# Two group norms whose statistics are taken where the image is written, and weights loaded by two queues

## The reference

```python
def _gn(v, G=16, eps=1e-5):
    g = v.reshape(B_, G, C_ // G, H_, W_)
    m = jnp.mean(g, axis=(2, 3, 4), keepdims=True)
    s = jnp.var(g, axis=(2, 3, 4), keepdims=True)
    return ((g - m) / jnp.sqrt(s + eps)).reshape(v.shape)

x = x + _L0_conv_ref(_gn(x), ...)   # attention over 16,384 pixels, one head of 48 channels
x = x + _L1_conv_ref(_gn(x), ...)   # 1x1 conv to 288 channels, 8x8 patch Fourier filter, 3x3 depthwise, GELU gate, 1x1
x = x + _L2_conv_ref(_gn(x), ...)   # state space scan over 4096 tokens of 192 features
x = x + _L3_conv_ref(_gn(x), ...)   # box means at learned offsets
```

## Time and profile before

| | |
|---|---|
| median of 3 runs | 7481.2 us (7479.07 to 7481.92) |
| profiled execution, its own time | 7482.72 us |
| its span in the trace | 7480.9 us |
| attention, units | 315 to 3119 us |
| block of the norm ahead of layer 1 (`gn1`) | 3121.9 to 3146.4 us |
| patch filter | 3146.4 to 3632.0 us |
| block of the norm ahead of layer 2 (`gn2`) | 3632.4 to 3657.9 us |
| DVE busy | 6842.5 us, 91% |
| PE busy | 6171.0 us, 82% |
| ACT busy | 5235.5 us, 70% |
| POOL busy | 3435.1 us, 46% |

### The profile page before, as it was taken

The page is one execution under the profiler, slowest core; times in us unless marked ns, Lnnn a source line. Parts: engine busy times, 40 slices in busy tenths (PEclk is TensorE's granted clock), DMA queues, the critical chain, the costliest instruction groups (busy, mean ns, idle before and its releaser), DMA issues. The chain is left out here.

```text
span 7480.9 us, 170231 instructions
## 1 busy us (share of the span) xinstructions
PE 6171.0 (82%) x69312; PEld 2683.0 (36%) x69312; DVE 6842.5 (91%) x6229; ACT 5235.5 (70%) x5309; POOL 3435.1 (46%) x1811
## 2 busy tenths in 40 slices
PE   6899999999999999799668888888888888866330
PEld 3333333333333333366323333333333333333220
DVE  7799999999999999899779999999999999986776
ACT  3388888888888888633468888888888888842000
POOL 2000000000000000100169999999999999974777
PEclk9899999999999999899889999999999999987665
DMA  2200000000000000000110000000000000022333
GB/s 42 61 8 8 8 11 8 8 8 8 8 11 8 8 8 8 4 0 0 45 49 6 6 6 6 6 6 6 6 6 6 6 6 6 6 57 74 83 84 81
DMA packets 129089, 146.51 MB, mean 20 GB/s; under 512 B 52077, under 2 KB 111245, under 8 KB 127261
## 3 DMA queue, kind: packets, MB, share of 16 engines
q1 hardware_dynamic: 102848, 82.30, 4.1%
q0 software_dynamic: 24576, 50.36, 2.6%
q10 hardware_dynamic: 960, 3.74, 0.3%
HBM read 98.55 MB, written 37.75 MB: 18 GB/s over the span
## 5 line engine op out<-in xcount | busy, mean ns | idle before, releaser
L1753 POOL TENSOR_TENSOR k_image<-k_image,s_b 128x1024 f32<-128x1024 f32 x1152 | 2700.6, 2355 | 117.9 <-ACT k_image L1666 83.3
L705 ACT ACTIVATE att_prob<-att_scores,a_bound,a_temp 128x1024 f32<-128x1024 f32 x2048 | 2354.8, 1201 | 421.9 <-PE att_scores L648 421.9
L716 DVE TENSOR_TENSOR att_prob_lo<-att_prob 128x1024 f16<-128x1024 f32 x2048 | 2431.9, 1237 | 157.3 <-ACT att_prob L705 141.7
L633 POOL TENSOR_TENSOR k_image<-k_image,att_rden 48x512 f32 x32 | 67.7, 2115 | 2987.5 <-DVE att_rden L728 2987.5
L1666 ACT COPY k_image<-h_du 128x1024 f32<-128x1024 f32 x1152 | 1166.2, 1012 | 322.5 <-PE h_du L1600 321.9
L1716 DVE TENSOR_TENSOR_SCAN h_state_odd<-h_keep,k_image 128x1024 f32<-128x1024 f32 x576 | 1366.2, 2470 | 0.0
L648 PE MATMUL att_scores<-att_queries,att_keys 32*128 32x512 f16 (+1 forms) x20480 | 1294.2, 378 | 21.4 <-DMA att_queries<-qk_halves 18.8
L1672 ACT ACTIVATE h_keep<-h_keep,h_decay 128x1024 f32<-128x1024 f32 x1152 | 1256.7, 1091 | 74.7 <-PE h_keep L1589 51.0
L665 PE MATMUL att_sums<-att_prob,a_values 128*64 128x512 bf16 x8192 | 1125.4, 395 | 0.0
L1589 PE MATMUL h_keep<-h_rows,h_spread 128*128 128x512 bf16 x2304 | 698.8, 385 | 511.8 <-DVE h_state_odd L1716 263.2
L1600 PE MATMUL h_du<-h_rows,h_spread 128*128 128x512 bf16 x2304 | 701.2, 386 | 37.0 <-DMA h_rows<-parts 34.8
(11 more groups left out here) (296 smaller groups left out, 7026.6 us busy)
## 6 DMA issues: line engine op xcount, KB each, us to landing
y_rows<-h_y_sb SPq DMA_DIRECT2D x1024, 3.0 KB
att_queries<-qk_halves SPq DMA_DIRECT2D x124, 128.0 KB, 2.2
parts<-t_part SPq DMA_DIRECT2D x48, 192.0 KB, 2.5
h_rows<-parts SPq DMA_DIRECT2D x128, 72.0 KB
b_shared<-cells,b_index POOLq DMA_INDIRECT x512, 2.6
qk_halves<-qkv_hi SPq DMA_DIRECT2D x128, 48.0 KB, 1.6
cells<-b_shared SPq DMA_DIRECT2D x4, 1536.0 KB, 5.1
att_keys<-qk_halves SPq DMA_DIRECT2D x32, 128.0 KB, 3.0
```

What stands on the lines that cost most here:

```text
L705: nc.scalar.activation(prob[:, u % RING, :], scores[:, u % SLOTS_S, :], ACT.Exp, bias=bound[:, 0:1], scale=temp[:, 0:1]).then_inc(prob_rea ...
L716: nc.vector.tensor_tensor(prob_lo[:, u % RING, :], prob[:, u % RING, :], prob_hi[:, u % RING, :], ALU.subtract).then_inc(low_ready, 1)
L1753: nc.gpsimd.tensor_tensor(drive[k % 3], du_sb[k % 3], b[:, c * CH:(c + 1) * CH], ALU.mult).then_inc(drive_ready, 1)
```

## The change

`group_norm` can now give ACT something to do before its square root (`first_scalar`) and after it (`last_scalar`). The buffer `stats` is allocated once for the program, and both norms get it filled.

In attention, DVE takes `bn_stats` of query block b-1 after unit 58 of block b, and of block 31 at the end. In the patch filter it takes two pieces per step just ahead of `mix(r, 1)` (one in step 2), one after each add of the tail, and one at the end. The image is stored to DRAM by SP during the patch filter, in 32 DMAs, each after its piece has been added, instead of in `gn2`. In `gn1`, 8 of the 16 weight DMAs go to ACT's queue, ACT builds the diagonals, the mask's factor 0.5 moves into a constant, and POOL waits for the masks alone.

```diff
@@ group_norm, ScalarE
+            if first_scalar is not None:
+                first_scalar(act)
             act.wait_ge(step, steps + 3)
             nc.scalar.activation(sd, var, ACT.Sqrt).then_inc(root, 1)
+            if last_scalar is not None:
+                last_scalar(act)
@@ attend, VectorE
+            def count(b):
+                dve.wait_ge(added, b + 1)
+                nc.vector.bn_stats(stats[HI, b, :], image[HI, b * BLK + W:(b + 1) * BLK + W]).then_inc(counted, 1)
+
             for u in range(ALL_UNITS):
                 low(u)
                 b, g = u // UNITS, u % UNITS
+                if b and g == COUNT_AT:
+                    count(b - 1)
...
+            count(NQB - 1)
+            dve.wait_ge(counted, NQB)
@@ patch_filter_layer, beside the norm
-            for dst, src in pairs:
-                sp.dma_start(dst, src).then_inc(loaded, 16)
+        def load_masks(sp):
+            for dst, src in ((mask[0:64, :], d["mask"]), (mask[64:P, :], d["mask"]), (mask2[0:64, :], d["mask_mirror"]),
+                             (mask2[64:P, :], d["mask_mirror"])):
+                sp.dma_start(dst, src).then_inc(masks_loaded, 16)
+            sp.dma_start(fwd[:, :], d["fourier_fwd"]).then_inc(loaded, 16)
             sp.wait_ge(cleared, 3)
             sp.dma_start(w_in[LO, :], d["w_in"]).then_inc(loaded, 16)
+            sp.dma_start(inv[:, :], d["fourier_inv"]).then_inc(loaded, 16)
+            sp.dma_start(w_oa[:, :], d["w_out"][0:P, :]).then_inc(loaded, 16)
+            sp.wait_ge(masks_loaded, 64)
+            sp.wait_ge(loaded, 16 * 11)
+
+        def load_taps(act):
+            act.dma_start(dwa[:, :], d["w_dw"][0:P, :]).then_inc(dwa_loaded, 16)
+            act.dma_start(dwb[:, :], d["w_dw"][HID:HID + P, :]).then_inc(loaded, 16)
+            act.wait_ge(cleared, 3)
...
+        def make_diagonals(act):
+            act.wait_ge(dwa_loaded, 16)
+            for t in range(TAPS):
+                nc.scalar.activation(diag[:, t, :], ident[:, :], ACT.Copy, scale=dwa[:, t:t + 1]).then_inc(made, 1)
+            act.wait_ge(made, 1 + TAPS)
@@ patch_filter_layer, SyncE during the layer
+            for j in range(2 * NPR):
+                sp.wait_ge(added, j + 2)
+                sp.dma_start(kept_image[:, j * BLK:(j + 1) * BLK], image[HI, W + j * BLK:W + (j + 1) * BLK]).then_inc(kept, 16)
@@ patch_filter_layer, VectorE
+            def count(j):
+                dve.wait_ge(added, j + 2)
+                nc.vector.bn_stats(stats[HI, ds(j, 1), :].rearrange("c a b -> c (a b)"),
+                                   image[HI, ds(j * BLK + W, BLK)]).then_inc(counted, 1)
...
                 for t in range(5, 7):
                     taps(k, kph, t)
+                if out:
+                    if not isinstance(r, int) or r > 2:
+                        count((r - 2) * 2 - 1)
+                    count((r - 2) * 2)
                 mix(r, 1)
...
                 for hh in range(2):
                     add(k, hh)
+                    count(k * 2 + hh - 1)
...
             add(NPR, 0, W)
-            dve.wait_ge(added, 2 * NPR + 1)
+            count(2 * NPR - 1)
+            dve.wait_ge(counted, 2 * NPR)
@@ project_tokens, beside the norm
-            for k in range(4):
-                px = slice(k * NPIX // 4, (k + 1) * NPIX // 4)
-                sp.dma_start(kept_image[:, px], image[HI, W + px.start:W + px.stop]).then_inc(kept, 16)
```

More of the change, by code:

```diff
@@ L206, with attention_layer @@
 INVERT_FROM = 18
+COUNT_AT = 58
 QUARTERS = [slice(W + k * NPIX // 4, W + (k + 1) * NPIX // 4) for k in range(4)]
-def attention_layer(nc, image, gmean, norm, sems, ident, d):
+def attention_layer(nc, image, gmean, norm, sems, ident, d, stats):
     with ExitStack() as layer:
@@ L229, in attention_layer @@
             project_qkv(nc, image, norm, ident, halves, values, x_split, qk_split, v_split, ones, least)
-        attend(nc, image, halves, values, out_w, bound, temp)
+        attend(nc, image, halves, values, out_w, bound, temp, stats)
 def load_and_prepare(nc, image, ident, d, x_split, qk_split, v_split, ones, least, stats, out_w, bound, temp):
@@ L574, in _, with attend @@
             root(nblk - 1)
-def attend(nc, image, halves, values, out_w, bound, temp):
+def attend(nc, image, halves, values, out_w, bound, temp, stats):
     with ExitStack() as ctx:
@@ L759, with patch_filter_layer @@
 TAPS_BESIDE = ((range(0, 2), range(2, 4)), (range(0), range(4, TAPS)))
-def patch_filter_layer(nc, image, gmean, norm, sems, ident, d):
+def patch_filter_layer(nc, image, gmean, norm, sems, ident, d, stats, kept_image, kept):
     with ExitStack() as ctx:
@@ L820, in prepare @@
             nc.gpsimd.memset(w_in[:, :], 0.0).then_inc(cleared, 1)
-            for t in (slab_a, slab_b, slab_c):
+            for t in (slab_a, slab_b):
                 nc.gpsimd.memset(t[:, :, :, :], 0.0).then_inc(cleared, 1)
-            nc.gpsimd.memset(gate_c[:, :], 0.0).then_inc(cleared, 1)
-            nc.gpsimd.memset(spec[:, :, :], 0.0).then_inc(cleared, 1)
-            pool.wait_ge(loaded, 16 * 16)
+            pool.wait_ge(masks_loaded, 64)
             nc.gpsimd.tensor_tensor(mask[:, :], mask[:, :], mask2[:, :], ALU.add).then_inc(made, 1)
-            pool.wait_ge(made, 1)
-            nc.gpsimd.tensor_scalar(mask[:, :], mask[:, :], 0.5, None, ALU.mult).then_inc(made, 1)
-            for t in range(TAPS):
-                nc.gpsimd.tensor_scalar(diag[:, t, :], ident[:, :], dwa[:, t:t + 1], None, ALU.mult).then_inc(made, 1)
-            pool.wait_ge(made, 2 + TAPS)
+            for t in (slab_c[:, :, :, :], gate_c[:, :], spec[:, :, :]):
+                nc.gpsimd.memset(t, 0.0).then_inc(cleared, 1)
             pool.wait_ge(cleared, 8)
-        group_norm(nc, "gn1", image, gmean, norm, sems, False, beside_sync=load_weights, beside_pool=prepare)
+        group_norm(nc, "gn1", image, gmean, norm, sems, False, beside_sync=load_masks, beside_pool=prepare,
+                   stats_ready=stats, first_scalar=load_taps, last_scalar=make_diagonals)
         ps_x = n.ps("ps_x", [C, 4, P])
@@ L1184, with scan_layer @@
 SIGMOID_1 = float(1.0 / (1.0 + np.exp(-1.0)))
-def scan_layer(nc, image, gmean, norm, sems, ident, d):
+def scan_layer(nc, image, gmean, norm, sems, ident, d, stats, kept_image, kept):
     parts = nc.dram_tensor("parts", [D, 2, 3, L], BF16, kind="Internal").ap()
@@ L2460, in program @@
         sems = NormSemaphores(nc)
+        stats = n.sb("stats", [P, NPIX // BLK, 6])
+        kept_image = nc.dram_tensor("kept_image", [C, NPIX], F32, kind="Internal").ap()
+        kept = n.sem("kept")
         with nc.cleanup_on_exit():
-            attention_layer(nc, image, gmean, norm, sems, ident, d)
-        patch_filter_layer(nc, image, gmean, norm, sems, ident, d)
-        rows = scan_layer(nc, image, gmean, norm, sems, ident, d)
+            attention_layer(nc, image, gmean, norm, sems, ident, d, stats)
+        patch_filter_layer(nc, image, gmean, norm, sems, ident, d, stats, kept_image, kept)
+        rows = scan_layer(nc, image, gmean, norm, sems, ident, d, stats, kept_image, kept)
         box_layer(nc, image, gmean, norm, sems, ident, d, out, *rows)
```

49 lines of the change are left out of this document (23 added, 26 removed).

## The result

| | before | changed |
|---|---|---|
| median | 7482.13 us (8 runs, 7479.07 to 7486.83) | 7459.77 us (8 runs, 7454.89 to 7466.89) |
| ratio, 95% interval | | 0.997 (0.9961 to 0.9979) |
| profiled execution: own time, span | 7482.72, 7480.9 us | 7462.4, 7460.1 us |

The change makes the kernel 0.3% faster, 22.4 us by the medians. The forecast was 7457.7 us.

The account below looks back on a forecast made before the run. DVE's statistics bound the first norm block, POOL waiting for weights behind the store also the second. Terms 0 + 0.8 - 15.7 + 3.6 + 3.5 - 15.7 = -23.5 gave 7459.2 us, median 7457.7, range 7450 to 7467.

Parts of the forecast that it names:

- Norm blocks, -15.7 each: Norms ahead of layers 1 and 2: blocks shrink from 24.55 to 8.8 and 25.46 to 9.7 us, POOL last in both.
- another engine keeps the norm blocks long: Rival, chance 0.06: DMAs or a queue hold both norm blocks at about half the gain, 7473 us.
- Attention, "Cost 0": Attention's 31 counts: each takes 0.83 us of DVE, but DVE catches up before the divisions, so they cost nothing.
- The +0.8 behind the last addition: Attention's end: the last count waits for POOL's last add and the barrier for the count, +0.8 us.
- Loop, +3.6: Patch filter's loop: two counts ahead of `mix(r, 1)` exceed DVE's wait, +0.27 us per step, +3.6 us in all.
- rival of counts that are not covered: Rival, chance 0.08: in the patch filter's loop 27 counts cost 19.4 us instead of 3.6; 7473.5 us, no measurable change.
- Tail, +3.5: Patch filter's tail: counts between adds delay bands 14 and 15 by 1.3 and 1.4 us, the last count 0.7.
- Store, cost 0: Storing the image early: 32 issues on SP's otherwise empty queue in the patch filter, nobody waiting, cost 0.
- Second queue, at most 1.4: Norm ahead of layer 1: by the skill's rule, splitting weight DMAs over two queues is worth at most some 1.4 us.
- rival of a scan that is paced otherwise: Rival, chance 0.05, either sign evenly: SBUF buffers move, later stages start at other times, some 20 us either way.
- The slower rival: Rival, chance 0.03: attention's count falls where PE is about to wait for the low half, 59 us over 31 blocks, 7517.
- its sum of bounds: All terms' ends together: -28.6 to -18.9 us, giving 7452 to 7463 us as the likeliest case's own range.

Follow-up runs that it names:

- e2: Changed kernel with the image's store put back into the norm block ahead of layer 2, four DMAs first on SP's queue: 7478.26 us, ratio 0.9993 to the kernel before.
- e3: Changed kernel with all 32 statistics of the norm ahead of layer 2 back in its own block, image still stored early: 7469.44 us, ratio 0.9983.
- e1: Changed kernel without statistics in attention; the norm ahead of layer 1 takes all 32 in its own block: 7476.47 us, ratio 0.999.
- e8: Changed kernel, attention's last count behind the last division; DVE builds diagonals and clears slab_c in first norm block, part of s_c_odd in second: 7459.11 us, ratio 0.9968.
- e9: e8 with ACT building the diagonals again, DVE clearing only slab_c there, three of ACT's eight DMA issues moved to SP: 7620.89 us, ratio 0.996 (kernel before 7650.55).
- e0: The kernel before, unedited, profiled once more: attention's first query DMA at 316.82 us, 1.35 us later than in its first profile.
- e7: Changed kernel with one count instead of two per step of the patch filter's loop, the other 13 at its end: 7467.9 us, ratio 0.9978.
- e4: Changed kernel with all 16 weight DMAs of the first norm block on SP again, ACT still building the diagonals: 7463.0 us, ratio 0.9972.
- e5: Changed kernel with the nine diagonals built on POOL again, two DMA queues kept: 7465.36 us, ratio 0.9975.
- e6: Changed kernel with attention's count behind unit 49 instead of 58: 7485.99 us, ratio 1.0002 to the kernel before.
- e10: Changed kernel, unedited, run again on the same chip as e9: 7625.24 us, ratio 0.9964 (kernel before 7650.55).

## Why the prediction was right, step by step

- **Norm blocks, -15.7 each: right** (-15.54, -15.75), and so was the claim that two things had to go in the second (e2, e3). In the first, ACT and not POOL is last, by 0.4 us: I took 3.7 us for its eight issues from the earlier trace rows, and they take 4.2 (4.20 to 4.22 us in all nine profiles that have them). SP issues beside ACT in both places, so that is not the difference; what lengthens them stays open. The nine activations were 0.2 us short as well. The rival "another engine keeps the norm blocks long" is out with these lengths.
- **Attention, "Cost 0": right inside, wrong at its end.** "It catches up some units later than before, far ahead of unit 18, where divisions begin again" is the step that failed. It holds for 30 blocks (e1, spacing), but in block 31 five units follow the count and then come the divisions. DVE carries its 0.83 us into them: +0.85. e1 takes it away, e8 and e9 recover it by moving the count. The +0.8 behind the last addition was right (0.75).
- **Loop, +3.6: right.** 0.26 per step and 3.5 us in sum, with the idle time, the overlap and the hold as argued. From the layer's first addition to band 14's it is 406.94 to 406.97 us in the kernel before, in e0, in e3 and in e7 with its one count per step, and 410.4 to 410.5 with two. That answers the rival of counts that are not covered: it asked for 19.4 us.
- **Tail, +3.5: right for the counts, 2.7 in the changed kernel's profile.** The counts cost what I said: the first pair 1.45 less 0.13 of slack, the second 1.45, the last one 0.72. But there PE answered 0.33 and 0.45 us sooner. The windows over the end of the filter (duration, busy time and count of PE, PEld, DVE, ACT and POOL, then the granted clock, DMA share, GB/s), e8 first, then the changed kernel:

```profile
3606.00:3612.00 6.00, 1.63 (x4) 0.00 (x0) 4.19 (x6) 2.54 (x5) 0.00 (x0) 0.78 0.12 33
3612.00:3618.00 6.00, 3.93 (x6) 0.69 (x6) 1.91 (x4) 0.00 (x0) 0.00 (x0) 0.50 0.01 3
3618.00:3627.00 9.00, 5.27 (x22) 4.56 (x22) 7.45 (x27) 0.58 (x2) 0.00 (x0) 0.50 0.08 23
```

```profile
3606.00:3612.00 6.00, 2.65 (x5) 0.24 (x4) 3.17 (x5) 2.54 (x5) 0.00 (x0) 0.50 0.10 28
3612.00:3618.00 6.00, 3.59 (x6) 0.69 (x6) 2.27 (x4) 0.00 (x0) 0.00 (x0) 0.62 0.02 4
3618.00:3627.00 9.00, 4.29 (x22) 3.88 (x22) 7.87 (x28) 0.59 (x2) 0.00 (x0) 0.80 0.08 22
```

The clock rises from its lower level (0.50, 1.2 GHz) for a while in both: in e8 while PE does little and nobody waits for it, in the changed kernel later, when DVE waits for PE (0.62 and 0.80 are means over stretches with both levels). PE's last products take 0.42 us there and 0.66 in e8. The profiles with counts in the tail fall into two groups. In e1, e4, e5 and e8 DVE waits 4.03 and 1.18 us as before the change, band 14's first addition to the last addition takes 18.7 us (15.95 before), and the tail costs the 3.5 us of the forecast. In the changed kernel, e2, e6, e7, e9 and e10 it takes 17.9 to 18.1 us, and the tail costs 2.7 to 2.9. The first group also starts the layer sooner, 61.7 to 61.9 us from the first activation to the first addition against 62.3 to 62.6, so that the whole filter differs by 0.4 us at most. So the 0.8 us hang on when the clock rises and not on the counts. What sets that moment is open. The first group has just the kernels whose first norm block is longer, 10.7 to 26.1 us against 8.5 to 9.0, but the kernel before needs 62.3 us at the layer's start behind a block of 24.5, so the length alone does not decide it, and no run varies it alone.
- **Store, cost 0: right** in the layer (e3), and where 0.25 us of it would show, at the end, the last count hides it. **Second queue, at most 1.4: too low,** 1.74 (e4), of which one slow issue in that profile is 0.67. The Trainium skill's rule named there says that a second queue saves issue time only; e4 agrees in that SP's issues ended the block. Whether the bytes move sooner no run here tests.
- **Later stages:** from DVE's first instruction of layer 2 to the end of the span it is 3822.3 us against 3823.0; e0 has 3820.8, and the experiments up to e8 have 3818.1 to 3825.5. The rival of a scan that is paced otherwise has nothing for it.
- **The slower rival** had the place and the mechanism right, and double the price (e6). Nine units between two places for the same instruction are worth more than the whole gain: behind unit 49 the kernel is no faster than before.

The sum of the changed stretches, -23.48, met the forecast of -23.5 better than the steps deserve, which is luck: +0.85 missed in attention and 0.8 less in the tail, from PE's clock, cancelled. (With the forecast's own terms the upper end of its sum of bounds is -18.8 and not -18.9; nothing follows from it.) The profiled execution came out 3.2 us above its forecast of 7459.2: 2.3 us of it the start of attention, 1.1 us in its first block and the spacing, which e0 and e10 show to vary as well, 0.5 us around the span, and 0.7 the other way in the later layers.

## What to carry to other kernels

Work moved beside other work is free only up to the wait that it fills, and only if something follows in which the engine catches up: look at the last iteration by itself. When two chains of equal length end a block, price neither alone. After such a gain the block's end belongs to whatever was second, here preparation on POOL and ACT, and that is the next thing to spread. And a term of under a microsecond is read from several profiles: the same instructions took 0.8 us more or less in the filter's tail by the moment at which PE's clock rose.

## What the hardware showed that I had not expected

- A DVE `tensor_scalar` of SBUF data, 0.28 us long, took 1.9 us beside POOL's memsets and ended 0.07 us after them; a DVE memset beside a POOL memset took its usual time (e8).
- A DVE `tensor_tensor` of one column, 0.16 us, took 0.36 beside POOL's mask addition in e9 and ended at 3128.53, 0.02 us after it. In the changed kernel the same instruction beside a POOL memset took 0.16. So POOL's addition held what its memset did not, each seen once.
- DMA issues do not all take the same time, and not for a reason that these runs show. Eight of ACT's took 3.7 us at attention's start and 4.2 us in the first norm block, with SP's queue issuing beside them both times. Single ones of 0.44 us took up to 0.79 (e3), one 1.26 (e9, both queues issuing), and one mask issue of 0.60 took 1.27 with SP issuing alone (e4).
- The granted clock of TensorE over the same work in the filter's tail was 0.78, 0.50, 0.50 in one execution (e8) and 0.50, 0.62, 0.80 in another (the changed kernel), in kernels whose instructions are alike there.
